# Identity matmuls between the uses of the bench and the units of maxima in the opening of an attention and local-attention kernel

## What is computed

```python
x = x + attn_block(_layernorm(x))    # 16 heads of 8 features; this is where the change lies
x = x + ffn_block(_layernorm(x))     # two layers of local attention and a gated MLP

# the core of attn_block, after a second layer norm
q, k, v = (einsum('bsd,dhf->bshf', x, W) for W in (Wq, Wk, Wv))
qb = softmax(einsum('bshf,hfn->bshn', q, Whq))      # 32 clusters a head
kb = softmax(einsum('bshf,hfn->bshn', k, Whk))
logits = einsum('bqhf,bkhf->bhqk', q, k) / sqrt(8) + 0.1 * einsum('bqhn,bkhn->bhqk', qb, kb)
out = einsum('bhqk,bkhf->bqhf', softmax(logits), v)  # then Wo, residual, layer norm, MLP of 512
```

## Time and profile before

| | |
|---|---|
| median of 3 executions | 1442.46 us (1438.47 to 1443.82) |
| profiled execution, its own time | 1443.05 us |
| span of the profiled execution | 1441.3 us, 27920 instructions |
| mean granted clock of TensorE | 0.964 of full speed |
| PE busy | 1268.8 us (88%) |
| DVE busy | 1084.5 us (75%) |
| ACT busy | 1007.7 us (70%) |
| POOL busy | 824.9 us (57%) |

### The profile page before, as it was taken

How to read it: one execution, slowest core, us unless ns; L and a number is a source line. 1 busy time by engine, 2 the same in 40 slices (tenths; PEclk the granted TensorE clock), 3 DMA queues, 4 the chain that set the end, 5 groups by cost and what they waited for, 6 DMA issues and landing times.

```text
span 1441.3 us, 27920 instructions
## 1 busy us (share of the span) xinstructions
PE 1268.8 (88%) x9636; PEld 643.8 (45%) x9636; DVE 1084.5 (75%) x1927; ACT 1007.7 (70%) x2327; POOL 824.9 (57%) x1020
## 2 busy tenths in 40 slices
PE   4489989899899977896799999988987999999898
PEld 1122222222222212365366666665434666666554
DVE  6678888888888865334499999994448999999644
ACT  4656767666676656774489999984348999999632
POOL 3466667676667631133778888860048787887100
PEclk9579999999999999998799999999999999999999
DMA  6533333333333320001111111120001111111001
GB/s 165 97 60 66 59 72 69 60 66 60 68 73 60 66 53 1 1 1 33 26 27 32 30 27 28 28 60 8 0 22 42 28 27 27 29 30 28 2 22 37
DMA packets 161119, 60.87 MB, mean 42 GB/s; under 512 B 139690, under 2 KB 152788, under 8 KB 160980
## 3 DMA queue, kind: packets, MB, share of 16 engines
q1 hardware_dynamic: 160980, 59.09, 19.3%
HBM read 8.60 MB, written 2.10 MB: 7 GB/s over the span
## 4 chain that ended last, share of the span: by engine, by line
PE 29%; ACT 11%; DVE 8%; issue 4%; POOL 2%; ACTq 0%; DVEq 0%; POOLq 0%
ACT la_s L1859 8%; PE la_ring L1480 6%; PE la_ring L1492 3%; PE la_s L1515 3%; PE la_pT L1589 3%; DVE la_prob L1748 2%; PE la_pT L1528 2%; PE la_m L1663 2%; PE la_ring L1577 2%; PE la_s L1579 1%; PE la_pT L1579 1%; PE la_s L1577 1%; ACT la_v_own L1901 1%; PE la_s L1507 1%; PE la_o L1544 1%
## 5 line engine op out<-in xcount | busy, mean ns | idle before, releaser
L785 DVE TENSOR_REDUCE row_max<-max_ps 128x2 f32<-128x1024 f32 x256 | 312.8, 1222 | 77.3 <-PE max_ps L481 75.8
L890 ACT ACTIVATE prob<-scores_ps 128x1024 f32<-128x1024 f32 x256 | 261.8, 1023 | 145.3 <-PE scores_ps L459 141.8
L1859 ACT ACTIVATE la_s<-la_s,la_bias,la_inv 128x128 f32<-128x128 f32 x512 | 223.2, 443 | 7.0 <-DVE la_bias L1736 7.0
L2010 POOL TENSOR_TENSOR la_turned<-la_raw,lw_rot 128x1024 f32<-128x1024 f32 x64 | 150.8, 2356 | 117.1 <-PE la_ring L1492 72.1
L1480 PE MATMUL la_ring<-lw_wqkv,la_hT 128*128 128x512 f32 x384 | 202.6, 638 | 15.5 <-DVE la_swapped L1711 6.8
L459 PE MATMUL scores_ps<-stack 128*128 128x512 f16 x512 | 155.7, 386 | 36.6 <-ACT prob L890 36.2
L2016 POOL TENSOR_TENSOR la_turned<-la_turned,la_swapped 128x1024 f32<-128x1024 f32 x64 | 150.6, 2354 | 5.0
L495 PE MATMUL heads_ps<-prob,XT 128*32 128x512 f32 x1024 | 137.9, 611 | 0.0
L481 PE MATMUL max_ps<-stack 24*128 24x512 f16 x512 | 102.7, 398 | 31.1 <-DVE row_max L785 19.1
L459 PEld LDWEIGHTS scores_ps<-stack 128*128 128x128 f16 x512 | 34.5, 97 | 203.8 <-ACT prob L890 148.9
L1067 POOL TENSOR_TENSOR cl<-cl,cl_inv 128x512 f32<-128x512 f32 x60 | 62.8, 1047 | 103.3 <-DVE cl_inv L691 103.3
(11 more groups left out here) (186 smaller groups left out, 2748.7 us busy)
## 6 DMA issues: line engine op xcount, KB each, us to landing
la_v_back<-la_v_own SPq DMA_DIRECT2D x112, 128.0 KB, 2.3
X<-in_x SPq DMA_DIRECT2D x8, 256.0 KB, 5.0
stack<-stack_tok SPq DMA_TRANSPOSE x128, 3.2
out<-X SPq DMA_DIRECT2D x8, 256.0 KB, 2.3
lw_wqkv<-in_wqkv SPq DMA_DIRECT2D x2, 768.0 KB, 4.3
lw_rot<-in_rot SPq DMA_DIRECT2D x2, 512.0 KB, 5.6
stack<-shift_row SPq DMA_DIRECT2D x64, 2.0 KB
lw_w<-in_fw SPq DMA_DIRECT2D x2, 341.0 KB
```

The source lines that it names most:

```text
L785: nc.vector.tensor_reduce(row_max[:, grp % 2, w // 2, :, w % 2], max_ps[:], AX.X, ALU.max).then_inc(max_made, 1)
L890: nc.scalar.activation(prob[:, c % 4, 2 * pr:2 * pr + 2, :], scores_ps[:], ACT.Exp, scale=1.0 / LOGIT_SCALE).then_inc(exp_made, 1)
L1859: ins = nc.scalar.activation(s_ps[:, place(h), :], s_ps[:, place(h), :], ACT.Exp, bias=bias[:, T % 2, h:h + 1], scale=inv[:, T % 4, h:h + ...
L2010: nc.gpsimd.tensor_tensor(spun, raw[:, T % 2].rearrange("p s (h f) -> p s h f", f=LD), rot[:, T % TPB, :, 0, :].unsqueeze(2).to_broadcast( ...
```

## The change

PE gets a helper `stay_busy` that issues WARMING = 4 matmuls: the stationary operand is the f16 identity, the moving operand is the same identity repeated four times to 512 columns, the output goes to the two banks of `scores_ps` in turn. Nothing reads that output. The helper is called behind every unit of maxima and behind every early use of the bench in slots -42 to -2. The first slot of this range is the one behind clq of tile 0, and PE's wait for the late loads, which bring `ident16`, is moved there from unit 0 of the maxima. The other engines and the DMA queue are unchanged.

```diff
--- before.py
+++ after.py
@@ -45,6 +45,7 @@
 ONE_BANK = MLP_SLOT - 3
 MC = MLP // P
 LOGIT_SCALE = 10.0
+WARMING = 4
 FEATURES = (96, 0)
 
 
@@ -464,8 +465,6 @@
 
                 b, g, w = u // SLOTS, u // UNITS % 4, u % UNITS
                 pair, qt, last = 2 * g + w % 2, w // 2, b * TPB + TPB - 1
-                if u == 0:
-                    pe.wait_ge(late_loaded, 16 * len(late_loads))
                 if g == 0 and w == 0:
                     pe.wait_ge(stack_made[1, 0], 16 * (last + 1))
                     pe.wait_ge(stack_made[0, 0], 16 * last)
@@ -540,12 +539,25 @@
                                                  shift_tok[:, qt], ident16[:])
                 mm.then_inc(bench_filled, 1)
 
+            def stay_busy():
+
+                for i in range(WARMING):
+                    nc.tensor.matmul(scores_ps[:, i % 2, :], ident16[:],
+                                     ident16[:].unsqueeze(1).to_broadcast([P, S // P, P]), start=True, stop=True)
+
             def slot(n):
                 s, (early, late) = streams(n), bench_uses(n)
+                if tile_at_step(n, 7) == 0:
+                    pe.wait_ge(late_loaded, 16 * len(late_loads))
+                unread = 7 - LEAD_PREP <= n < -LEAD_SCORES
                 if s["max"] is not None:
                     make_max_scores(s["max"])
+                    if unread:
+                        stay_busy()
                 for use in early:
                     fill_bench(use)
+                    if unread:
+                        stay_busy()
                 if s["pv"] is not None:
                     weight_values(s["pv"])
                 if s["scores"] is not None:
```

## The result

| | before | changed |
|---|---|---|
| median | 1441.43 us (4 executions) | 1462.15 us (1459.81 to 1463.78, 4 executions) |
| ratio, 95% interval | | 1.014 [1.012, 1.0159] |
| span of the profiled execution | 1441.3 us | 1462.0 us |
| unit 0 of the maxima starts at | 58.15 | 58.74 |
| unit 11 | 81.66 | 84.62 |

The kernel is 20.7 us slower, above the range that was given. Only 3.3 us of that is lost before unit 20, where the change is. The rest comes long after the last added matmul has run. The starts of the units are read from PE's and VectorE's timelines.

The account below looks back on a forecast made before the run. Until 91.20 us the maxima stage was seen as a serial chain of matmul pairs and row maxima at half clock. 1443.05 + 0 + 2.07 - 1.90 = 1443.2, for the median 1442.7 us; range 1439.0 to 1448.0.

Parts of the forecast that it names:

- No DMA or queue order moves.: Said of moving PE's wait for the late loads from unit 0 to slot -42; effect priced at 0.
- Rival D: Units 0 to 10: identity products do not lift the clock, or not in time; +15.5 us, 1458; chance 0.05.
- What the opening gains or loses is carried to the end: From 91.20 us, at full clock, slots follow each other in order, so the opening's gain or loss persists.
- The sum of the opening: Maxima stage 25.58 against 23.51 us, +2.07; slots -1 to 2 take 7.64 instead of 9.54, -1.90.
- Price of a burst: Four matmuls behind a unit or bench use cost PE 1.68 us at half clock, 0.85 at full.
- rival of a cheaper burst: Seven full-clock bursts on PE's path cost 0.33 us less each, net -2.1: 1440.4; chance 0.06.
- Before unit 0: Bursts behind bench uses before 58.15 us: taken as 0, ends -0.5 and +1.5, since each lateness has cover.
- rival E: Bench uses before 58.15 us become the path through VectorE's queue: +1 to +4, 1445; chance 0.07.
- The moved wait: PE's wait for late loads, moved to slot -42: at most 1 us of PE delay near 18 us, priced 0.
- Clock: Maxima stage: clock at 1.00 from about 62 us to the stage's end; four slots behind it also at full clock.
- rival C: Clock rises but falls back in slots -10 to -8; 3.6 us more: 1446.3; chance 0.12.
- Rival A: Full clock before 58.15 us, kept up by bursts in tiles 2 to 4; net -1.4: 1441.1; chance 0.06.

Follow-up runs that it names:

- count208: Changed kernel without bursts, 104 matmuls of 32 columns (208 instructions) in front of the first unit of maxima instead; 1457.75 us, ratio 1.0129.
- four_padded: Changed kernel plus 24 matmuls of 128 columns in front of the first unit of maxima, 256 added instructions in all; 1442.47 us, ratio 1.001.
- wait_only: Changed kernel with WARMING 0: no bursts, only the wait for the late loads stays moved to slot -42; 1439.55 us, ratio 0.9991.
- early_pad: Changed kernel with bursts behind the maxima units alone and 84 matmuls of 32 columns at slot -34; 1438.65 us, ratio 0.9991.
- max_only_88: Changed kernel with bursts behind the maxima units alone and no pad, 88 added instructions; 1439.95 us, ratio 0.9997.
- five: Changed kernel with WARMING 5: five matmuls per burst instead of four, 260 added instructions in all; 1445.56 us, ratio 1.003.
- max_only_256: Changed kernel with bursts behind the maxima units alone and 84 matmuls of 32 columns before the first unit, 256 added instructions; 1439.38 us, ratio 0.9999.
- padded_late: Changed kernel plus 24 matmuls of 128 columns in slot 128, in front of the scores; 1451.45 us, ratio 1.0078.
- count128: Changed kernel without bursts, 64 matmuls of 32 columns (128 instructions) in front of the first unit of maxima instead; 1453.91 us, ratio 1.0109.

## Why the prediction was wrong

- **The step that failed** is the sentence "No DMA or queue order moves." PE's own instructions come through a DMA queue, and what was added moved their blocks against the transposes. The 104 matmuls and 104 weight loads were priced by their time on PE alone (loads at nothing, "short loads beside PE"), and the term for their 208 places in the instruction stream was missing, that is, nothing. By count208, which has these places and next to none of the work, it is 1.29% of the time before, 18.6 us (interval 14.3 to 23.1; by the medians, 1457.75 and 1441.53, 16.2). In the trace of the change it shows as late transposes (about 9.4 us) and falls of the clock behind them (about 4.1). No rival had this; D named the right sign and a time of 1458 for a reason that did not happen.
- **"What the opening gains or loses is carried to the end"** held for the opening's 3.3 us: they are still there at unit 54. But it was read as if nothing else could be added on the way.
- **The sum of the opening** was right. With the shift of the blocks taken out (four_padded), the maxima stage takes 25.10 us against 25.58 forecast, the four slots after it 7.70 against 7.64, and the ratio is 1.001 [0.9995, 1.0026] where +0.2 us was forecast. It was right slot by slot, so this is no luck: from slot -12 on the slots took 2.04, 3.85, 1.71, 1.73, 1.71, 2.80, 1.80, 3.01, 1.71, 3.01 and 1.71 us, none more than 0.20 from its forecast. In the change itself the stage took 25.88, with the clock's rise at 63.9 where the forecast had about 62; the first two slots took 2.36 and 4.32 there. (In the last step of the sum, 1443.2 less 0.6 is 1442.6, not 1442.7, which changes nothing.)
- **Price of a burst:** 0.86 us at full clock (18.81 to 19.67 on PE's timeline), forecast 0.85; 1.82 at half clock (59.28 to 61.10), forecast 1.68. The rival of a cheaper burst is out; the Trainium skill's 131 ns (TensorE: Matmul & The Clock Gate, Back-to-back issue gap) is not what these streams show: 0.86 us for four is 215 ns each.
- **Before unit 0:** right in size (58.74 against 58.15), partly by luck: in the runs without a block near these transposes unit 0 starts at 56.7 to 58.2 (wait_only, early_pad, max_only_88, and before), in the others at 58.2 to 58.8. Every run with bursts behind the bench uses has a block among the transposes between 46 and 60 us, so how much of this is the block's and how much that of rival E (late bench uses) stays open. The moved wait costs nothing, as forecast, although PE's wait for the late loads near 18 us, named as a sign of being wrong, did appear: PE idled 1.25 us, and tile 2's transpose still started at 17.99 against 17.94 before.
- **Clock:** it rose, at 63.9 (forecast about 62). It fell at 87.8, in the slots behind the last burst, which the forecast did not have; rival C had a fall, of another place. At unit 15 the loss was 3.2 us where 0.2 was forecast, and 2.1 of the 3.0 between them are this fall (9.78 us for the four slots, not 7.64); in four_padded and five the clock stayed up there. Rival A (full clock before unit 0) is out for the change: the clock was at 0.50 from 53.6 to 63.9.
- **Rival D** (the identity does not lift the clock) is out: 64 to 87 us ran at full clock.

The Trainium skill (Runtime: NRT & Kernel Launch, section Instruction fetch mechanics) says that instructions are refilled by DMA in blocks of 16 KiB, 256 instructions, and that crossing a block is mostly hidden. The block size agrees with the 16 KB packets and with the return of the old time at 256 and 260 instructions. Whether the crossing is hidden for PE itself, no run here settles; for a transposing DMA on the critical path it is not, by 0.9 to 1.8 us of landing each time (4.1 to 5.0 against 3.2).

What stays open: it is not settled why the clock falls at an idle in one run and not in another. The slots behind the opening have idles of 0.36, 0.69 and 0.79 us in the change and in four_padded alike, and the clock fell in the change (and near there in max_only_256) and not in four_padded or five. The same holds for the idles of 2.30 and 1.70 us at units 246 and 249: the clock fell at both in the change, in padded_late and in early_pad, at the first alone in wait_only and four_padded, at none in the kernel before, five and max_only_88. Which of the 16 DMA engines carries the block, and whether a transpose could be kept off it, was not tried.

## What to carry to other kernels

Adding or removing instructions on a long-running engine shifts where its instruction blocks are fetched. Where short DMAs are on the path, a kernel with an equal count modulo 256 (padded to it with small matmuls) is the fair one to compare with, before the edit itself is judged; a few other counts may do as well, as the 88 of max_only_88 did. Steps of delay at a fixed interval, long after an edit's own place, are a reason to look for this first. To keep a clock up, one might cover the slots up to the one in which real work takes over; no run here tried that.

## What was not expected of the hardware

- One 16 KB packet of instructions among the small packets of a transposing DMA (668 of under 512 bytes in the 2 us shown) makes it land in 4.4 us instead of 3.2 (4.1 to 5.0 over all of them), and the chain behind it (GpSimd's cast, VectorE's sum, the maxima, PE) passes on 0.9 to 1.7 us each time.
- The 2.00 us of idle that this gives PE was followed by a fall of the clock from 1.00 to 0.50 for 3.4 us, another 1.0 to 1.6 us each of the three times that this happened. In the profiled execution of count128 the same lateness at other tiles brought no fall.
- An idle of PE of 2.30 us, at the same place of the work, left the clock at 1.00 in the kernel before and was followed by 3.4 us at 0.50 in the changed kernel.
- Twenty-four matmuls whose output nobody reads changed 1462.15 us into 1442.47.
